# Row maxima taken in pieces of 370 keys, in two PSUM banks, with three banks for the score tiles

## What is computed

```
q = lat @ Wq;  k, v = split(concat([ctx, lat]) @ Wkv)          # lat: normalised x
attn = softmax(q k^T * 64**-0.5)                                 # 1024 x 1101 for each head
x = x + concat_heads(attn v) @ Wout
x = x + shared(h) + routed(h)                                    # h: normalised x
```

## Time and profile before

| | |
|---|---|
| median of 3 runs | 1611.84 us (1609.86 to 1613.97) |
| profiled execution | 1614.24 us, of which the span of its instructions is 1612.5 us |
| TensorE (PE) busy | 1503.6 us, 93% of the span |
| VectorE (DVE) busy | 1043.6 us, 65% |
| GpSimd (POOL) busy | 940.4 us, 58% |
| ScalarE (ACT) busy | 796.2 us, 49% |
| row-maximum reductions, L1325 | 256, 1305 ns in the mean, 334.1 us busy |
| row-maximum matmuls, L927 | 768, 357 ns in the mean, 190.7 us busy |
| granted TensorE clock | 0.984 in the mean |

### The profile page before, as it was taken

How to read it: one execution, slowest core, us unless ns; L and a number is a source line. 1 busy time by engine, 2 the same in 40 slices (tenths; PEclk the granted TensorE clock), 3 DMA queues, 4 the chain that set the end, 5 groups by cost and what they waited for, 6 DMA issues and landing times.

```text
span 1612.5 us, 23811 instructions
## 1 busy us (share of the span) xinstructions
PE 1503.6 (93%) x8086; PEld 1059.1 (66%) x8086; DVE 1043.6 (65%) x1574; ACT 796.2 (49%) x1501; POOL 940.4 (58%) x751
## 2 busy tenths in 40 slices
PE   4799999999999999999999999988989999999995
PEld 4465665555655665566555565546889999999995
DVE  6557556676676665767767776556756666666662
ACT  3455445444554455444554445433436666666663
POOL 4567756666677676765768768882534333343333
PEclk9999999999999999999999999998999999999998
DMA  3034430000000000000001011002256666666664
GB/s 107 11 81 96 101 81 15 10 15 10 25 15 10 15 11 24 15 11 15 24 18 32 24 41 33 31 31 69 87 172 189 178 168 176 182 189 180 168 177 90
DMA packets 99282, 117.93 MB, mean 73 GB/s; under 512 B 10595, under 2 KB 78181, under 8 KB 99173
## 3 DMA queue, kind: packets, MB, share of 16 engines
q1 hardware_dynamic: 82149, 96.97, 20.6%
q0 software_dynamic: 17056, 19.97, 6.3%
HBM read 74.93 MB, written 35.06 MB: 68 GB/s over the span
## 4 chain that ended last, share of the span: by engine, by line
PE 75%; DVE 16%; POOL 3%; ACT 3%; issue 2%; DMA 1%; SPq 0%; DVEq 0%; POOLq 0%; ACTq 0%
PE ps_o L965 14%; PE ps_t L822 9%; PE ps_m L822 8%; PE ps_m L927 8%; PE ps_st L822 7%; DVE arena_r L1325 7%; PE ps_st L950 6%; PE ps_st L954 6%; PE ps_m L859 3%; PE ps_o L859 3%; PE ps_t L985 2%; PE ps_t L1032 2%; PE ps_t L972 2%; DVE arena L1336 2%; POOL arena L762 2%
## 5 line engine op out<-in xcount | busy, mean ns | idle before, releaser
L762 POOL TENSOR_TENSOR arena<-arena 128x512 f32<-128x512 f32 (+1 forms) x512 | 660.8, 1292 | 321.7 <-ACT arena L1608 284.0
L1608 ACT ACTIVATE arena<-ps_st 128x512 f32<-128x512 f32 (+1 forms) x576 | 330.0, 597 | 457.5 <-PE ps_st L954 444.8
L1325 DVE TENSOR_REDUCE arena_r<-ps_m 128x1 fp32r<-128x1107 f32 x256 | 334.1, 1305 | 189.2 <-PE ps_m L927 187.0
L797 POOL DMA_INDIRECT acc_rows<-arena,ids x96 | 150.8, 1570 | 268.2 <-ACT arena L1671 240.5
L965 PE MATMUL ps_o<-arena 128*64 128x512 f32 (+1 forms) x1152 | 275.2, 603 | 0.0
L950 PE MATMUL ps_st<-arena_r 128*128 128x512 f32 (+1 forms) x576 | 246.3, 428 | 2.7 <-ACT arena L1608 2.6
L954 PE MATMUL ps_st<-arena_r 68*128 68x512 f32 (+2 forms) x576 | 230.8, 401 | 3.2 <-DVE arena_r L1332 2.1
L927 PE MATMUL ps_m<-arena_r 128*128 128x370 f32 x768 | 190.7, 357 | 36.4 <-DVE arena_r L1325 32.6
L927 PEld LDWEIGHTS ps_m<-arena_r 128*128 128x128 f32 x768 | 131.0, 191 | 102.2 <-DVE arena_r L1325 84.0
L950 PEld LDWEIGHTS ps_st<-arena_r 128*128 128x128 f32 (+1 forms) x576 | 106.6, 185 | 102.3 <-ACT arena L1608 68.2
L822 PE MATMUL ps_m<-arena_r 128*128 128x320 f32 (+1 forms) x864 | 165.2, 327 | 2.1 <-DVE arena_r L1415 1.2
(11 more groups left out here) (212 smaller groups left out, 1860.1 us busy)
## 6 DMA issues: line engine op xcount, KB each, us to landing
arena<-in_L_ffn_wg_dram SPq DMA_DIRECT2D x32, 512.0 KB, 4.6
arena<-in_L_ffn_wu_dram SPq DMA_DIRECT2D x32, 512.0 KB, 6.0
arena<-in_L_ffn_wd_dram SPq DMA_DIRECT2D x32, 512.0 KB, 3.9
x_slots<-route SPq DMA_DIRECT2D x5, 2176.0 KB, 12.9
arena<-x_slots SPq DMA_DIRECT2D x32, 272.0 KB, 2.7
arena_r<-arena_r SPq DMA_DIRECT2D x30, 275.2 KB, 3.6
arena<-in_L_xattn_Wkv_dram SPq DMA_DIRECT2D x32, 128.0 KB, 2.4
arena<-x_slots SPq DMA_DIRECT2D x32, 68.0 KB, 2.4
```

The lines of the kernel that those rows point to most:

```text
L762: pool.tensor_tensor(total, probsT[0:rows, h, 0, :] if kt == 1 else total, probsT[0:rows, h, kt, :], ALU.add).then_inc(added, 1)
L797: pool.indirect_dma_start(out=dst[:, :], in_=y_sb[par][:, c, 0:w], in_offset=None, compute_op=ALU.add, out_offset=bass.IndirectOffsetOnAxi ...
L1325: dve.tensor_reduce(neg[h][:, c:c + 1], ps_m[:, :, 0:PIECE_W], AX.XY, ALU.max, negate=True)\
L1608: act.activation(probsT[0:rows, h, kt, :], ps_st[0:rows, n % 2, :], ACT.Exp).then_inc(exp_done, 1)
```

## The change

- The reduction over three banks becomes three over one bank each: a `max` event (now six for a head, not four) takes two pieces of 370 columns, each into its own of the two banks of `ps_m`, with its own wait and its own count on `max_ready` and `max_done`. The twelve pieces of a head go to `piece_max`, and a new event `neg` reduces them to the four negated columns; `row` waits for `neg_done`.
- The third bank goes to `ps_st`: a score tile waits for the exponential of the third tile before it, not the second. Scratch uses of the third bank of `ps_m` move along (`ey_bank`, `route_bank`, `zc_bank`).
- The places in the slots change: six `max` events and `neg` for four `max` events; `last_values` now stand together; `k_low[0]` stands ahead of the second `own_max`, and `q_low` stays in slot (0, 5), behind or ahead of the last `own_max` as the lines show.

```diff
@@ -44,6 +44,7 @@
...
+MAX_STEPS = 6
@@ -80,34 +81,35 @@
         first_values = values(own, d, (0, 1, 2))
         more_values = values(own, d, (3, 4, 5))
         last_values = values(old, prev, (6, 7, 8))
-        own_max = [own("max", d, 1, i) for i in range(4)]
-        next_max = [nxt("max", n, 0, i) for i in range(4)]
+        own_max = [own("max", d, 1, i) for i in range(MAX_STEPS)] + [own("neg", d, 1)]
+        next_max = [nxt("max", n, 0, i) for i in range(MAX_STEPS)] + [nxt("neg", n, 0)]
         out = [old("out", prev, i) for i in range(2)]
         after = {(0, 8): [own("row", d, 1), old("sum", prev)],
                  (1, 1): [next_max[0]],
                  (1, 2): [old("norm", prev)],
                  (1, 3): first_values + [next_max[1]],
                  (1, 4): [out[0], next_max[2]],
-                 (0, 7): last_values[2:]}
+                 (1, 5): [next_max[3]]}
         if project:
-            after[0, 0] = [own_max[0]] + project_k(0) + [own_max[1], k_low[0]]
+            after[0, 0] = [own_max[0]] + project_k(0) + [k_low[0]]
+            after[0, 1] = [own_max[1]]
             after[0, 2] = project_k(2) + [own_max[2], k_low[2]]
-            after[0, 3] = project_k(1) + [k_low[1]]
-            after[0, 4] = [own_max[3]]
-            after[0, 5] = project_q() + [q_again] + last_values[:2] + [q_low]
+            after[0, 3] = project_k(1) + [own_max[3], k_low[1]]
+            after[0, 4] = [own_max[4]]
+            after[0, 5] = project_q() + [q_again] + last_values + [q_low] + own_max[5:]
             after[1, 5] = [nxt("v", pp, 0), next_max[3]]
-            after[1, 6] = more_values + [nxt("row", n, 0), out[1]]
+            after[1, 6] = next_max[4:5] + more_values + next_max[5:] + [out[1], nxt("row", n, 0)]
             after[1, 7] = [nxt("v", pp, 1)]
             after[1, 8] = [nxt("v", pp, 2)]
         else:
-            after[0, 0] = [own_max[0], nxt("q", pp, n % 2)]
-            after[0, 1] = [own_max[1], q_high[0]]
+            after[0, 0] = [own_max[0]]
+            after[0, 1] = [nxt("q", pp, n % 2), own_max[1], q_high[0]]
             after[0, 2] = [q_high[1]]
             after[0, 3] = [own_max[2]]
-            after[0, 4] = last_values[:2] + q_high[2:]
-            after[0, 5] = [own_max[3], q_low]
-            after[1, 6] = [out[1], next_max[3]]
-            after[1, 7] = more_values + [nxt("row", n, 0)]
+            after[0, 4] = [own_max[3]] + last_values + [own_max[4]] + q_high[2:]
+            after[0, 5] = own_max[5:] + [q_low]
+            after[1, 6] = [out[1], next_max[4]]
+            after[1, 7] = next_max[5:] + more_values + [nxt("row", n, 0)]
         if d == 0:
             after[1, 1] = [own("w", 1)] + after[1, 1]
         if d == 2:
@@ -220,8 +222,8 @@
...
               ("lo", "k", 0, 2), ("max", 0, 0, 0), ("v", 0, 0), ("bstat", 0), ("v", 0, 1), ("broot", 0),
-              ("max", 0, 0, 1), ("bstat", 1), ("v", 0, 2), ("broot", 1), ("max", 0, 0, 2), ("max", 0, 0, 3),
-              ("row", 0, 0)]
+              ("max", 0, 0, 1), ("max", 0, 0, 2), ("bstat", 1), ("v", 0, 2), ("broot", 1), ("max", 0, 0, 3),
+              ("max", 0, 0, 4), ("max", 0, 0, 5), ("neg", 0, 0), ("row", 0, 0)]
@@ -338,10 +340,12 @@
...
-    MAX_T = O_T * 8
+    MAX_H = 2 * MAX_STEPS
+    MAX_T = O_T * 2 * MAX_H
+    NEG_T = O_T * 2
...
-    assert PIECE_W >= PIECE and PIECE_W % 2 == 1 and PIECE_W < 512
+    assert PIECE_W >= PIECE and PIECE_W % 2 == 1 and 2 * MAX_STEPS == 4 * KEY_PIECES and PIECE_W < 512
@@ -471,6 +475,7 @@
...
+        piece_max = sb("piece_max", [P, 4, KEY_PIECES])
@@ -492,14 +497,14 @@
...
-        ps_m = stack.enter_context(nc.psum_tensor("ps_m", [P, 3, 512], F32))
-        ps_st = stack.enter_context(nc.psum_tensor("ps_st", [P, 2, 512], F32))
+        ps_m = stack.enter_context(nc.psum_tensor("ps_m", [P, 2, 512], F32))
+        ps_st = stack.enter_context(nc.psum_tensor("ps_st", [P, 3, 512], F32))
...
-        ey_bank = (ps_o, ps_m[:, 2, :])
-        route_bank = (ps_m[:, 2, :], ps_o[:, :])
+        ey_bank = (ps_o, ps_st[:, 2, :])
+        route_bank = (ps_st[:, 2, :], ps_o[:, :])
...
-        zc_bank = ps_m[:, 2, :].rearrange("p (k n) -> p k n", k=DT)
+        zc_bank = ps_st[:, 2, :].rearrange("p (k n) -> p k n", k=DT)
@@ -548,7 +553,7 @@
...
-            return T * ST_T + SCORES.index(("st", d, h, kt)) + 1 + 2
+            return T * ST_T + SCORES.index(("st", d, h, kt)) + 1 + 3
@@ -920,16 +925,15 @@
...
-                    pe.wait_ge(max_done, T * MAX_T + d * 8 + h * 4 + i + 1)
-                    c = d % 2 * 512 + i * P
-                    for piece in range(KEY_PIECES):
-                        lo = piece * PIECE
-                        mm = pe.matmul(ps_m[:, piece, 0:PIECE_W + 1], q1[h][:, c:c + P], k1[pp][h][:, lo:lo + PIECE_W + 1],
-                                       start=True, stop=True)
-                    mm.then_inc(max_ready, 1)
+                    for bank_m, piece in enumerate((2 * i, 2 * i + 1)):
+                        pe.wait_ge(max_done, T * MAX_T + (d * 2 + h) * MAX_H + piece + 1)
+                        c = d % 2 * 512 + piece // KEY_PIECES * P
+                        lo = piece % KEY_PIECES * PIECE
+                        pe.matmul(ps_m[:, bank_m, 0:PIECE_W + 1], q1[h][:, c:c + P], k1[pp][h][:, lo:lo + PIECE_W + 1],
+                                  start=True, stop=True).then_inc(max_ready, 1)
...
                     _, d, h = ev
-                    pe.wait_ge(max_done, T * MAX_T + d * 8 + h * 4 + 4 + 1)
+                    pe.wait_ge(neg_done, T * NEG_T + d * 2 + h + 1)
@@ -947,11 +951,11 @@
...
                     pe.wait_ge(exp_done, T * ST_T + n + 1)
-                    pe.matmul(ps_st[0:rows, n % 2, :], k1[pp][h][:, r], q1[h][:, c:c + 512],
+                    pe.matmul(ps_st[0:rows, n % 3, :], k1[pp][h][:, r], q1[h][:, c:c + 512],
...
-                    pe.matmul(ps_st[0:rows, n % 2, :], k2[pp][h][kr, r], q2[h][kr, c:c + 512],
+                    pe.matmul(ps_st[0:rows, n % 3, :], k2[pp][h][kr, r], q2[h][kr, c:c + 512],
@@ -1072,7 +1076,7 @@
...
-            dve.sem_inc(max_done, 1)
+            dve.sem_inc(max_done, 2)
@@ -1320,10 +1324,16 @@
                     ins.then_inc(free, 1)
                 if kind == "max":
                     _, d, h, i = ev
-                    dve.wait_ge(max_ready, T * MAX_T + d * 8 + h * 4 + i + 1)
-                    c = MROW[h].start + i
-                    dve.tensor_reduce(neg[h][:, c:c + 1], ps_m[:, :, 0:PIECE_W], AX.XY, ALU.max, negate=True)\
-                       .then_inc(max_done, 1)
+                    for bank_m, piece in enumerate((2 * i, 2 * i + 1)):
+                        dve.wait_ge(max_ready, T * MAX_T + (d * 2 + h) * MAX_H + piece + 1)
+                        dve.tensor_reduce(piece_max[:, piece // KEY_PIECES, piece % KEY_PIECES:piece % KEY_PIECES + 1],
+                                          ps_m[:, bank_m, 0:PIECE_W], AX.X, ALU.max).then_inc(max_done, 1)
+                if kind == "neg":
+                    _, d, h = ev
+                    dve.wait_ge(max_done, T * MAX_T + (d * 2 + h + 1) * MAX_H + 2)
+                    c = MROW[h].start
+                    dve.tensor_reduce(neg[h][:, c:c + 4], piece_max[:, :, :], AX.X, ALU.max, negate=True)\
+                       .then_inc(neg_done, 1)
                 if kind == "row":
                     _, d, h = ev
                     r = MROW[h]
@@ -1506,7 +1516,7 @@
...
-            act.sem_inc(exp_done, 2)
+            act.sem_inc(exp_done, 3)
@@ -1605,7 +1615,7 @@
...
                     act.wait_ge(st_ready, T * ST_T + n + 1)
-                    act.activation(probsT[0:rows, h, kt, :], ps_st[0:rows, n % 2, :], ACT.Exp).then_inc(exp_done, 1)
+                    act.activation(probsT[0:rows, h, kt, :], ps_st[0:rows, n % 3, :], ACT.Exp).then_inc(exp_done, 1)
```

More of the change, by code:

```diff
@@ L531, in xattn_moe @@
         w_hi_ready, w_split, pair_hi = (sem(n) for n in ("w_hi_ready", "w_split", "pair_hi"))
-        max_ready, max_done = sem("max_ready"), sem("max_done")
+        max_ready, max_done, neg_done = sem("max_ready"), sem("max_done"), sem("neg_done")
         st_ready, exp_done = sem("st_ready"), sem("exp_done")
```

## The result

The changed kernel takes 1704.09 us in the median of four runs (1699.42 to 1705.76), the kernel before 1612.74 us beside it: a ratio of 1.056 (1.0545 to 1.0573), 91 us slower. Slower was forecast, and the mechanism too; the size was not: 62 us were foreseen, and the range ended at 1692. The profiled execution took 1703.34 us, with a span of 1701.6.

The account below looks back on a forecast made before the run. TensorE in its fixed order was the path, stopping wherever VectorE was late; 2.0 + 0.6 + 0.5 + 0.9 = 4.0 us per pair of blocks, 64 in 16 pairs, less 2, gave +62: 1674 us, range 1642 to 1692.

Parts of the forecast that it names:

- hand-made schedule of the odd block: Attention blocks that also project keys and values: low parts done at 5.39 us, fifth piece waits 1.56 to 6.01.
- the even block's first half: Attention, even block up to the `sum` matmul: short distances and `sum` waiting for `lo q`, net +0.5 us.
- even block, second half: Attention, even block after `sum`: output adds stand between pieces and delay the fourth and last maximum, net +0.9 us.
- separate value group: Value matmuls in attention: `last_values` now run together, so one separate group goes, 0.35 us taken away.
- odd block, first half: Attention, odd block up to `row`: `lo k0` and `lo q` ahead of maxima, added 3.2, taken away 1.18, net +2.0 us.
- odd block, second half: Attention, odd block after `row`: about 0.5 us taken away; short distances, a refill and `neg` added, net +0.6 us.
- short distance of pieces 8 and 9: Odd block, second half: these pieces come one score tile behind 6 and 7, before their banks are free, 0.54 us.
- Third score bank: Score tiles in attention: worth between 2.7 and 68.2 us; low end taken, some 0.1 us per block.
- The pieces come in time: Rival: VectorE's other work does not get ahead of the reductions, banks free after 0.54 us; 1597 us, 7%.
- No overlap: Rival: VectorE's pieces do not overlap, 0.57 us each, about 0.9 us more per pair; 1688 us, 12%.
- cheap pieces: Rival: VectorE's pieces take 0.39 us, so the short distances vanish; 34 us lost in all, 1646 us, 8%.
- the third bank pays in full: Rival: at the score tiles the third bank gains 68 us against 62 lost; 1606 us, 4%.

Follow-up runs that it names:

- The run with the additional matmuls: Changed kernel with five repeated score-tile matmuls more in every odd block, just ahead of the fifth piece: 1696.33 us, 1.0514.
- Pieces alone: Kernel before, its order and banks kept, with only the reduction cut in three, each piece with its own wait and count, and `neg`: 1596.78 us, 0.9896.

## Why the prediction was right and wrong

**Right: the bound and the mechanism.** TensorE's order is the path, and VectorE's order decides. The hand-made schedule of the odd block holds to 0.05 us up to the stop: low parts done after 5.39 us, fifth piece at 6.02 against 6.01. A piece takes 0.534 us (0.536 worked out); two take 0.99 (577.19 in the odd block), so the second starts 0.46 after the first (0.45). `neg` takes 0.166. `row` waits 0.73 (0.72), `sum` 0.53 (0.6), the pieces behind the adds 0.54 and 0.60 (0.6 each); the even block's first half gives 0.44 (0.5).

The Trainium skill ("VectorE: DVE Perf Modes", section on the TRN2 errata) states the fixed cost by which the prediction estimated 509 ns for a piece, and advises tiles of 512 elements or more, there against the latency of SBUF. The measured 534 agrees in kind with the estimate. The advice does not decide here: pieces of 369 alone made the kernel 1.0% faster, since VectorE was not the bound.

**Wrong: even block, second half, 0.9 predicted and 2.03 measured.** The stops behind the adds were right. What failed is the count of what the change moves: the step priced the separate value group as time saved, 0.35 us, and looked no further. It moves ScalarE's copy and the high parts ahead of four exponentials, and from there GpSimd's adds, `norm` and `out`. The prediction never followed GpSimd, which was 58% busy and had no stop of TensorE to its name in the rows shown. Its price is 0.95 us per even block at `out`, 15 us in 16; moving the high parts alone gave back 10 us in all. It is the largest single miss.

**Wrong: odd block, first half, 2.0 and 2.55.** The stop itself was right; the clock that falls behind it was no term of the sum. The eight odd blocks without a fall take 17.56 us, 1.9 more than before, so the waits came out as worked out. The seven with it take 1.4 more each, 10 us in all or 0.67 per odd block, and that is the whole of this miss. The run with the additional matmuls bears it out.

**Too small: odd block, second half, 0.6 and 0.95**, 6 us in all. It is not the short distance of pieces 8 and 9, which costs 0.44 there with its refills (0.54 predicted). At `out` 0.16 more is again GpSimd's. The rest I can't assign.

**Third score bank: some 3 us taken, 10 measured**; this miss went the other way. Of the two ends, 2.7 and 68.2, the low one was right for the waits, and the 10 is nearly all clock, which was again no term.

The three misses make 1.13 + 0.55 + 0.35 us for a pair, 32 in 16 pairs, against 29 missing; the ends of attention cost less than the middle. My pair of blocks, 63.4 us, was also 2.0 shorter than the mean of 15 pairs, but the differences held for the means.

**The rivals.** "The pieces come in time" was 7% and false for this change; it had the right point, the place of `lo k0`, but not its second condition, a bank for each piece of a step. Pieces alone meet both, and they came out at 1597, its number, if partly by chance: that kernel wins at stops at maxima, the rival had them at `sum` and the adds. The Trainium skill ("Perfetto Trace Analysis", section on optimizing Scalar/DVE operations) says that breaking up the instructions of an engine that isn't saturated but holds up others may let work finish sooner. Both signs are here: 1.0% faster with three banks, and with two banks in the same order 20% slower. "No overlap" (1688) falls by the 0.46 us between two starts, "cheap pieces" by the 0.534 of one; "the third bank pays in full" by the 10 us of the run without it.

## What to carry to other kernels

Cutting a consumer's instruction in pieces paid here as long as each piece of a step kept a bank of its own; with a bank fewer, the producer waited for whatever the consumer had ahead in its queue, and not for the piece. When a list of events is reordered, follow every moved event on every engine that executes a part of it, to the place where its result is wanted, including engines that look idle: here ScalarE's order reached TensorE twelve microseconds later through GpSimd. And where two chains end at the same place, removing one wait shows nothing, so count a stop as a loss only up to the next one. When two kernels differ by a per cent, compare blocks without a fall of the clock apart from those with one, before a cause is named: the 10 us of the third score bank looked like waits and were not.

## What the runs showed of the hardware

- A stop of TensorE can cost more than its length. After 1.60 us without work in a stretch that was otherwise dense, the granted clock fell from 1.00 to 0.50 for 3.4 us, and six matmuls of 512 columns took 2.69 us, not 1.57; a fall cost 1.4 us (18.99 against 17.56). The same stop stands in fifteen odd blocks, but only seven of them show the fall, and with the stop filled to 0.45 us none does. The kernel with pieces alone has five such stretches without that stop, all in even blocks. What decides it was not settled here.
- Reductions of 0.53 us that are ready start 0.46 us after one another: two take 0.99, three 1.44 us. The low parts do not overlap so: two of 0.684 take 1.39.
